# A two-half pipeline of a metaformer kernel: the combine of half 0 placed at other slots beside the second expert layer of half 1

## The reference, cut to what matters

```
probs = softmax(hs @ router_gate.T)
topk_scores, topk_idx = top_k(probs, 2); topk_scores /= sum(topk_scores)
h = up * silu(gate)                      # gate, up = x @ expert_gate_up[e]
out_rows = h @ expert_down[e]
out[token] += out_rows * score           # two rows per token
t = t + out                              # then back to channels x positions
```

## Time and profile before

| | before |
|---|---|
| median of 3 runs | 1376.64 us (1374.26 to 1381.2) |
| the profiled execution | 1379.38 us |
| its span | 1377.6 us |
| PE busy | 1071.1 us (78%) |
| DVE busy | 755.8 us (55%) |
| ACT busy | 491.5 us (36%) |
| POOL busy | 441.9 us (32%) |
| mean DMA rate | 163 GB/s |

### The profile page before, as it was taken

How to read it: one execution, slowest core, us unless ns; L and a number is a source line. 1 busy time by engine, 2 the same in 40 slices (tenths; PEclk the granted TensorE clock), 3 DMA queues, 4 the chain that set the end, 5 groups by cost and what they waited for, 6 DMA issues and landing times. The chain is left out here.

```text
span 1377.6 us, 17796 instructions
## 1 busy us (share of the span) xinstructions
PE 1071.1 (78%) x5842; PEld 893.4 (65%) x5842; DVE 755.8 (55%) x1350; ACT 491.5 (36%) x993; POOL 441.9 (32%) x308
## 2 busy tenths in 40 slices
PE   7434798658979996588767995997599688889964
PEld 4323778648878786478766674786478566667853
DVE  5376674677756747777673445753543233333325
ACT  3320432523234335234603436255223233333332
POOL 1112234343345344444313334333124222223310
PEclk9656899879989998798878998999799899999985
DMA  9300443623447444245416454445444667666439
GB/s 296 123 0 10 128 145 109 196 76 117 133 139 216 116 152 137 78 136 179 169 61 255 153 199 179 162 145 198 155 142 138 227 245 264 246 220 231 184 131 327
DMA packets 111202, 224.43 MB, mean 163 GB/s; under 512 B 9940, under 2 KB 71860, under 8 KB 101388
## 3 DMA queue, kind: packets, MB, share of 16 engines
q1 hardware_dynamic: 76824, 139.57, 30.9%
q0 software_dynamic: 13760, 45.10, 9.5%
q10 hardware_dynamic: 20532, 38.61, 8.0%
HBM read 156.60 MB, written 66.66 MB: 162 GB/s over the span
## 5 line engine op out<-in xcount | busy, mean ns | idle before, releaser
L527 PE MATMUL ps<-sb_xnH,sb_ring 128*128 128x288 f32 x512 | 169.5, 331 | 26.4 <-DVE sb_xnL L1371 16.9
L494 POOL DMA_INDIRECT y_dram<-sb_ysb,sb_target x86 | 85.4, 993 | 323.6 <-ACT sb_ysb L1001 319.9
L472 POOL TENSOR_TENSOR sb_ring<-sb_raw,sb_ring 128x1024 fp32r<-128x1024 f32 x48 | 120.0, 2501 | 210.1 <-ACT sb_ring L930 210.1
L1424 DVE TENSOR_TENSOR sb_xtL<-ps,sb_xtH 128x512 fp32r<-128x512 f32 x86 | 59.4, 691 | 179.6 <-ACT sb_xtH L981 171.0
L737 PE MATMUL ps<-sb_w,sb_xtH 128*128 x344 | 154.8, 450 | 1.8 <-DVE sb_hh L1431 0.7
L528 PE MATMUL ps<-sb_xnH,sb_ring 128*128 128x288 f32 x512 | 154.7, 302 | 0.0
L529 PE MATMUL ps<-sb_xnL,sb_ring 128*128 128x288 f32 x512 | 154.2, 301 | 0.0
L739 PE MATMUL ps<-sb_w,sb_xtH 128*128 x344 | 138.9, 404 | 0.0
L738 PE MATMUL ps<-sb_w,sb_xtL 128*128 x344 | 138.3, 402 | 0.0
L527 PE MATMUL ps<-sb_itH,sb_ring 128*128 128x288 f32 x256 | 95.5, 373 | 38.5 <-DVE sb_X L1389 20.1
L527 PEld LDWEIGHTS ps<-sb_xnH,sb_ring 128*128 128x128 f32 x512 | 100.5, 196 | 35.4 <-issue 30.6
(11 more groups left out here) (207 smaller groups left out, 2445.8 us busy)
## 6 DMA issues: line engine op xcount, KB each, us to landing
sb_w<-w_dram SPq DMA_DIRECT2D x48, 1024.0 KB
sb_raw<-in_w_ffn SPq DMA_DIRECT2D x96, 256.0 KB, 5.2
w_dram<-sb_stage SPq DMA_DIRECT2D x24, 1024.0 KB, 5.0
sb_raw<-in_w_ffn SPq DMA_DIRECT2D x24, 512.0 KB, 3.7
sb_X<-in_x SPq DMA_DIRECT2D x16, 576.0 KB, 8.8
xn_dram<-sb_XN ACTq DMA_DIRECT2D x18, 512.0 KB, 3.1
sb_g<-y_dram ACTq DMA_DIRECT2D x18, 512.0 KB
out_x<-sb_X ACTq DMA_DIRECT2D x16, 576.0 KB
```

What stands on the lines that cost most here:

```text
L472: pool.tensor_tensor(to[:, 1, :], raw[:, r % 2, :], to[:, 0, :].bitcast(f32), ALU.subtract)\
L494: pool.indirect_dma_start(y_dram[h], bass.IndirectOffsetOnAxis(ap=target[:, h, m:m + 1], axis=0), ysb[:, r, :], None).then_inc(y_stored[r] ...
L527: pe.matmul(out_ap, w[0], xh, start=start, stop=False)
L1424: v.tensor_tensor(xtL[:, i % 2, :, :], PS[:, 0, :].rearrange("p (k n) -> p k n", n=P), xtH[:, i % 2, :, :].bitcast(f32), ALU.subtract).the ...
```

## The change

In PE's combine the transposes of tile t go from slot at + 4t + 2 to at + 4t + 8. In DVE's combine the pieces go from slot at + 4t + 2 to at + 4t + 3, and a piece now holds the weighted sum of tile t and the add of tile t-2, where it held the add of tile t-1; the loop is one longer. ACT, POOL and SP are unchanged. The same functions serve the combine of half 1 after the loop.

```diff
@@ PE @@
             def combine(h, at):
                 for t in range(TL):
-                    yield at + 4 * t + 2
+                    yield at + 4 * t + 8
                     n = h * TL + t
                     pe.wait_ge(gt_ready, n + 1)
@@ DVE @@
             def combine(h, at):
-                for t in range(TL + 1):
-                    yield at + 4 * t + 2
+                for t in range(TL + 2):
+                    yield at + 4 * t + 3
                     n = h * TL + t
                     if t < TL:
                         v.wait_ge(gs_ready, n + 1)
...
-                    if t:
-                        v.wait_ge(f_ready, n)
-                        dst = X[:, :, tile_of(h, t - 1)]
-                        v.tensor_tensor(dst, dst, PS[:, 4 + (n - 1) % 4, :].rearrange("p (k n) -> p k n", n=P),
+                    if t >= 2:
+                        v.wait_ge(f_ready, n - 1)
+                        dst = X[:, :, tile_of(h, t - 2)]
+                        v.tensor_tensor(dst, dst, PS[:, 4 + (n - 2) % 4, :].rearrange("p (k n) -> p k n", n=P),
                                         ALU.add).then_inc(f_added, 1)
```

## The result

The changed kernel takes 1342.1 us (median of 4 runs, 1338.0 to 1344.3), where the kernel before, measured with it, takes 1375.5 (4 runs, 1371.4 to 1381.2); the ratio is 0.975, 95% interval 0.971 to 0.979. The forecast was 1340, range 1331 to 1355. The profiled execution took 1342.08 us with a span of 1340.3, 37.3 us less than the profiled execution before; the medians are 33.3 us apart.

The account below looks back on a forecast made before the run. PE was taken to set the time, losing some beside the combine. Steps 3 to 25 gave -37.9 us and the tail +1, total -36.9: profiled 1379.4 becomes 1342.5, the median 1339.7, said as 1340 us; range 1331 to 1355.

Parts of the forecast that it names:

- (d): ACT's output stores in the loop wait for the later add and delay the work behind them: 2.0 us lost.
- (e): Start of the combine: step 3 of half 1 starts some 4.0 us earlier, 1.9 us lost again to slow clock.
- (a): PE's transposes come five slots after DVE's sum: waits at line 771 go, with all 38.6 us of excess.
- (b): DVE's sum and add lie together, 1.43 us; before h_lo they cost near 0.05 us, six times: 0.3 us.
- (f): Loads, gathers, puts and expert weights: bytes and order unchanged, slack remains; nothing added for the denser DMA traffic.
- (g): Tail, combine of half 1: ACT's stores wait for the later add; +1 us taken, bounds nothing and 10 us.
- rival of the slow clock: PE's short waits beside the combine keep it at 1.2 GHz, steps 9.6 instead of 4.81 us: 1445 us; chance 0.04.

Follow-up runs that it names:

- e1_pe3: Changed kernel with PE's transposes at slot at + 4t + 3, the same slot as DVE's sum, instead of at + 4t + 8: 1365.2 us, ratio 0.992.
- e2_pe5: Changed kernel with PE's transposes at slot at + 4t + 5, two slots behind DVE's sum instead of five: 1343.0 us, ratio 0.976.
- e4_store: Changed kernel with each output store one tile later in ACT's order, in the loop and the tail: 1340.0 us, ratio 0.973.
- e8_pe4: Changed kernel with PE's transposes at slot at + 4t + 4, one slot behind DVE's sum: 1347.2 us, ratio 0.979.
- e7_pe5_lag1: Changed kernel with PE's transposes two slots behind DVE's sum and the add one step behind it, in loop and tail: 1341.1 us, ratio 0.974.
- e3_tail: Changed kernel with the add one step behind again only in the combine after the loop (half 1): 1342.3 us, ratio 0.976.

## Why the prediction was right, step by step

The forecast took 36.9 us off; the profiled executions, from which it was built, are 37.3 apart: 3.2 us by the start of step 3, 34.3 from there to step 28, and 0.2 lost again in what follows. That the parts agree this well is partly luck: two terms, of (d) and (e), were wrong by over a microsecond each and in opposite directions, and the runs of one kernel differ by several us. One row was misread: the 120.2 us of the earlier trace rows count the matmuls' wait of 52.6 us and the weight loads' of 67.6 together, so the text's "120.2 us in all" is over twice PE's idle time at line 771; the sum did not use them, since it was built from step starts.

**(a) The waits before line 771.** Put at 38.6 us of excess over steps 3 to 25. Measured 36.0 less, with the new stalls of (d) in it. e1_pe3 shows that it is PE's place behind the sum: with it taken back, the waits return, and with them part of the slow clock (a mean of 0.97; 0.94 before, 1.00 after), and 22.7 of the 34.3 us are lost. What the prediction left unsaid is that the rest of the change, with PE no further behind the sum than before, is worth a third of it.

**(b) DVE's block.** Put at 0.3 us with PE's transposes as cover (0.05 a step), 2.4 without (six times 0.4). e2_pe5 took the cover away: six steps 0.4 us longer, 2.4 us more of waits, 1.97 us of time in the stretch. With the cover, and no store before it, such a step takes 5.29 to 5.31 us where its neighbours with transposes take 5.24 to 5.27 (e4_store).

**(d) ACT's stores.** Put at 2.0 us; e4_store shows 3.3. The mechanism and the two worst steps (t = 8 and 17) were right, the size of these two was half: I had ACT free at the end of the add, and the issue of the store itself holds ACT for 0.38 us more before h_hi. A step so held lost 1.05 us, not 0.5.

**(e) The start.** The 4.0 us that step 2 gives were right (17.2 to 13.3). The 1.9 us of slow clock in step 3 were not. The half microsecond in which the clock returned from 0.50 to 1.00, before the change, in the changed kernel and in e8_pe4, one row each, in the columns of the earlier trace rows:

```profile
1087.00:1087.50 0.50, 0.50 (x3) 0.37 (x2) 0.00 (x0) 0.00 (x0) 0.00 (x0) 0.66 0.00 0
```

```profile
1085.00:1085.50 0.50, 0.50 (x4) 0.48 (x3) 0.00 (x0) 0.30 (x2) 0.00 (x0) 0.73 0.00 0
```

```profile
1087.50:1088.00 0.50, 0.50 (x4) 0.42 (x3) 0.15 (x1) 0.04 (x1) 0.26 (x1) 0.85 0.81 172
```

So the clock was full again at about 1085.3, and step 3 lost 0.4 us. I had taken over 6.4 us after the restart; before the change it was in fact 5.9 (1081.48 to 1087.3), and now it was 3.5 (1081.73 to 1085.3). PE now restarts on matmuls instead of transposes, but this alone does not explain it: e8_pe4 restarts on the same matmuls (at 1081.66, its first combine transposes at 1084.39) and needed 6.0 us. Why it was sooner is open, and the 1.5 us that it saved against the forecast are luck. They and the 1.3 us of (d) nearly cancel.

**(f) The DMA.** The denser mix runs at a share of 0.85 and 306 GB/s, at 0.98 and 363 GB/s over 22 us, and PE does not wait for it in this stretch of the changed kernel; in e7_pe5_lag1, with the same traffic, it did once, for 1.6 us. The rate of the old stretch was a rate of demand, not a bound. The Trainium skill, page SBUF — State Buffer, section "A bandwidth-pool intuition that's wrong (but worth ruling out)", has about 358 GB/s as a core's share of HBM; here one core ran alone and moved 363 GB/s over 22 us and 395 over ten in e1_pe3, so the figure was no ceiling.

```profile
1170.00:1180.00 10.00, 9.22 (x47) 7.11 (x46) 3.91 (x7) 3.75 (x8) 3.98 (x4) 1.00 1.01 395
```

**(g) The tail.** Put at +1, bounds 0 and 10; measured 0.1 by the tail's length, and e3_tail shows 0.3 at most. The reason, that loads release ACT there, was right: with the adds out of the way ACT waited for loads instead.

The rival of the slow clock did not come: with waits of 0.2 to 0.8 us in e8_pe4 and of 0.2 to 1.2 us in e2_pe5 the mean clock of the stretch is 0.99 and 1.00. That the clock can be lost by the combine's waits is shown by e1_pe3.

## What to carry to other kernels

Where work of a second stream is laid beside a loop by hand-written slots, place each consumer so many slots behind its producer that it comes after the work the producer's engine must do first; here two slots, one less than a step, were enough for the sum itself, and the mean clock says at once whether the waits also cost speed. Compare the times of like steps and not the waits alone. Then look at every in-order engine for pieces that wait on that chain (a store, a first load): they are not on the path, but what stands behind them is. Moving such pieces later gave another 12 us here, at no price that the runs show.

## What the runs showed of the hardware that was not expected

A wait that the profile puts at 0.2 us before a PE instruction costs about 0.4 us in its step, before line 771 in e8_pe4 (5.69 for 5.25 us) and before line 756 in e2_pe5 (5.73 for 5.30). In a stream a matmul is shown 0.39 us long and the next one starts 0.23 us after it; in e8_pe4 line 771 starts 0.62 us after the last line 758 (1106.41 to 1107.03), 0.39 more than in the stream, of which the bracket shows only 0.23. In e8_pe4 the next step is 0.3 us longer as well; what holds it was not looked into. The issue of one 576 KB store occupies ACT for 0.38 us during which no activation starts (1139.97 to 1140.45). The same wait of 1.59 us before line 771 occurs in e1_pe3 with the mean clock of its ten us at 0.83 (1130 to 1140) and at 1.00 (1160 to 1170, 7.96 us busy), in steps of 8.48 and 7.75 us. The steps with this wait alternate there, 7.62, 8.48, 7.75, 8.44 and 7.69 us (the start at 1105.17 comes first), while before the change each took 8.55 to 8.74: whether a wait of this length loses the clock is not set by its length alone. What sets it was not tried.
